# Convolution by taps: the fourth tap of 5 of 14 tiles a chunk goes from VectorE to ScalarE and GpSimd

## What is computed

```python
def _short_conv(x, w):                       # 4 taps, causal, per channel
    xp = jnp.pad(x, ((0, 0), (cs - 1, 0), (0, 0)))
    y = sum((xp[:, i:i + t, :] * w[:, i] for i in range(cs)))
    return jax.nn.silu(y)

q = _short_conv(x @ Wq, conv_q)              # 8 heads of 128 channels
k = _short_conv(x @ Wk, conv_k)              # 3 x 8 heads
v = _short_conv(x @ Wv, conv_v)              # 3 x 8 heads
# per token, 3 Householder steps of the state S (128 x 128 a head), then o = q S
S = S * jnp.exp(gt)[..., None, None]
for i in range(nh):
    kS = jnp.einsum('bhd,bhde->bhe', ki, S)
    S = S + bi[..., None, None] * (ki[..., None] * (vi - kS)[:, :, None, :])
```

## Time and profile before

| | |
|---|---|
| three runs | 8217.16, 8217.32, 8226.03 us (median 8217.32) |
| profiled execution | 8217.97 us, its span 8215.9 us |
| busy, share of the span | TensorE 90%, VectorE 79%, ScalarE 67%, GpSimd 50% |
| mean granted TensorE clock | 0.944 of full |
| stretches | 0 to about 150 us preparation; then the attention to about 6900 us; then the experts |
| one iteration of the loop (8 chunks) | 218.42 us |

### The profile page before, as it was taken

How to read it: one execution, slowest core, us unless ns; L and a number is a source line. 1 busy time by engine, 2 the same in 40 slices (tenths; PEclk the granted TensorE clock), 3 DMA queues, 4 the chain that set the end, 5 groups by cost and what they waited for, 6 DMA issues and landing times. The chain is left out here.

```text
span 8215.9 us, 426591 instructions
## 1 busy us (share of the span) xinstructions
PE 7423.3 (90%) x155940; PEld 6296.7 (77%) x155940; DVE 6459.2 (79%) x22300; ACT 5469.5 (67%) x20343; POOL 4117.8 (50%) x6333
## 2 busy tenths in 40 slices
PE   5889999999999999999999899999989999889999
PEld 3777777777787777777777777777777777757777
DVE  4888888888888888888888888888888888623333
ACT  3777777777777777777777777777777777533333
POOL 0555555555555555555555555555555555511111
PEclk6899999999999999999999999999999999889999
DMA  2000000000000000000000000000000000010000
GB/s 90 8 10 9 10 9 10 9 10 9 10 10 9 10 10 10 9 10 9 10 9 10 9 10 9 10 9 10 10 9 10 9 10 10 7 32 8 10 8 8
DMA packets 283626, 97.69 MB, mean 12 GB/s; under 512 B 226097, under 2 KB 276545, under 8 KB 281153
## 3 DMA queue, kind: packets, MB, share of 16 engines
q1 hardware_dynamic: 281408, 68.93, 3.8%
HBM read 52.08 MB, written 16.78 MB: 8 GB/s over the span
## 5 line engine op out<-in xcount | busy, mean ns | idle before, releaser
L819 DVE SCALAR_TENSOR_TENSOR CY<-PP,CWV,CY 128x128 f32<-128x128 f32 x4608 | 1585.5, 344 | 148.6 <-ACT CY L736 68.7
L819 DVE SCALAR_TENSOR_TENSOR CY<-PP,CWK,CY 128x128 f32<-128x128 f32 x4608 | 1581.4, 343 | 98.0 <-ACT CY L736 24.3
L1031 POOL TENSOR_TENSOR UM<-U,C 32x256 f32<-32x256 f32 x1536 | 1104.8, 719 | 120.2 <-POOL UM L1031 19.6
L1024 POOL TENSOR_TENSOR Y<-U,C 32x256 f32<-32x256 f32 x768 | 554.0, 721 | 1075.6 <-DVE UQ L912 1035.4
L550 PE MATMUL PI<-T,WB 32*32 32x32 f32 x49152 | 749.6, 196 | 303.2 <-DVE T L828 301.1
L550 PEld LDWEIGHTS PI<-T,WB 32*32 32x32 f32 x49152 | 639.0, 111 | 466.3 <-issue 403.2
L530 PE MATMUL PP<-XT,WV 128*128 128x131 f32 x3072 | 750.8, 328 | 188.5 <-issue 124.7
L530 PE MATMUL PP<-XT,WK 128*128 128x131 f32 x3072 | 783.6, 340 | 81.3 <-DVE CY L819 81.2
L736 ACT ACTIVATE CY<-PP,CWK 128x128 f32<-128x128 f32 x1536 | 564.4, 367 | 398.5 <-PE PP L530 387.4
L1004 POOL TENSOR_TENSOR S<-R,BETA 96x4 f32<-96x4 f32 x512 | 101.3, 198 | 1392.4 <-DVE R L872 1392.2
L736 ACT ACTIVATE CY<-PP,CWV 128x128 f32<-128x128 f32 x1536 | 567.2, 369 | 339.3 <-PE PP L530 328.0
(11 more groups left out here) (228 smaller groups left out, 18910.8 us busy)
## 6 DMA issues: line engine op xcount, KB each, us to landing
EX<-exd SPq DMA_DIRECT2D x768, 32.0 KB
exd<-EXS SPq DMA_DIRECT2D x16, 512.0 KB, 2.6
XR<-in_L_attn_x SPq DMA_DIRECT2D x65, 64.0 KB, 3.1
XL<-in_L_attn_x SPq DMA_DIRECT2D x16, 256.0 KB, 2.8
XRES<-in_L_attn_x SPq DMA_DIRECT2D x64, 64.0 KB, 2.7
x<-X SPq DMA_DIRECT2D x64, 64.0 KB, 3.1
XI<-x SPq DMA_DIRECT2D x16, 256.0 KB, 2.9
out<-OUT SPq DMA_DIRECT2D x16, 256.0 KB, 2.3
```

Source lines behind the costliest of these rows:

```text
L819: dve.scalar_tensor_tensor(CY[:, m % RING], ptile(m)[:, s:s + P], taps_of(m)[:, s:s + 1], CY[:, m % RING], ALU.mult, ALU.add).then_inc(tap ...
L1024: pool.tensor_tensor(Y1[r, :, :], U[r, par, :, r], over(first[r, :], [BK, NHEAD, BK], 1), ALU.mult).then_inc(seed_sb, 1)
L1031: pool.tensor_tensor(UM[r, lv], U[r, par, :, r], over(merge[lv][r, :], [BK, NHEAD, BK], 1), ALU.mult).then_inc(made, 1)
```

## The change

Of the 14 tiles of a chunk, those of slots 0, 1, 5, 6 and 7 (`OFF`) lose VectorE's third step. ScalarE makes tap 3 times its weight out of PSUM into a new ring buffer `CZ` of four tiles, just ahead of the instruction that makes `CY`. VectorE's tap 2 then counts for two on `taps_sb`. GpSimd adds `CZ` to `CY` (`last_tap`), and ScalarE's silu of these tiles waits for that (`tap3_sb`). GpSimd's additions stand at three places of its chunk: tile 0 after `YF` and `RS`; tile 1 after `FB`; tiles 5, 6 and 7 after `RT` and ahead of the wait for `UQ`.

```diff
+OFF = (0, 1, 5, 6, 7)
+NOFF = len(OFF) * CPS
...
+        ZRING = 4
+        assert NOFF % ZRING == 0
+        CZ = sb("CZ", [P, ZRING, P])
...
+        tap3_sb = sem("tap3_sb")
...
+        def off_rank(m):
+
+            return len(OFF) * (m // SLOTS) + OFF.index(m % SLOTS)
...
                             need(act, kqv_sb, T - RING + 1)
+                            if k in OFF:
+                                act.activation(CZ[:, off_rank(m) % ZRING], ptile(m)[:, 3:3 + P], ACT.Copy, scale=taps_of(m)[:, 3:4])
                             act.activation(CY[:, m % RING], ptile(m)[:, 0:P], ACT.Copy, scale=taps_of(m)[:, 0:1]).then_inc(tap0_sb, 1)
...
-                            act.wait_ge(taps_sb, 3 * (T + 1))
+                            if m % SLOTS in OFF:
+                                act.wait_ge(tap3_sb, NOFF * j + off_rank(m) + 1)
+                            else:
+                                act.wait_ge(taps_sb, 3 * (T + 1))
...
-                                             ALU.mult, ALU.add).then_inc(taps_sb, 1)
+                                             ALU.mult, ALU.add).then_inc(taps_sb, 2 if s == 2 and m % SLOTS in OFF else 1)
...
-                        if taps:
+                        if taps and m % SLOTS not in OFF:
                             tap(j, m, 3)
...
+                def last_tap(i, m):
+                    pool.wait_ge(taps_sb, 3 * (TILES * i + m + 1))
+                    pool.tensor_tensor(CY[:, m % RING], CY[:, m % RING], CZ[:, off_rank(m) % ZRING], ALU.add).then_inc(tap3_sb, 1)
...
+                    if known(i, 0, NSC):
+                        for k in OFF:
+                            if k in (0,):
+                                last_tap(i, SLOTS * c + k)
                     if c == 2 and known(i - 2, 0, NSC):
...
+                            if k in (1, 2):
+                                last_tap(i, SLOTS * c + k)
                     if do_prep:
...
                         pool.tensor_tensor(RT[:, :], SSE[:, :], half4[:, :], ALU.pow).then_inc(rt_sb, 1)
+                    if known(i, 0, NSC):
+                        for k in OFF:
+                            if k in (5, 6, 7):
+                                last_tap(i, SLOTS * c + k)
+                    if do_prep:
                         pool.wait_ge(u_sb, 2 * prep + 2)
```

## The result

| | before | with the change |
|---|---|---|
| median | 8215.61 us (20 runs) | 8237.47 us (20 runs) |
| profiled execution | 8217.97 us | 8232.63 us |
| ratio, same chip | | 1.0026, 95% interval 1.0015 to 1.0038 |
| on a second chip | 8239.56 us (23 runs) | 8243.41 us (12 runs): 1.0004, 0.9993 to 1.0015 |

The change costs 22 us on one chip, which can be told there, and 4 us, nothing that can be told, on the other. The forecast was 8229 us, +0.14%.

A forecast was written before the change was run, and what follows sets the result against it. VectorE was taken to pace TensorE until slot 3, ScalarE from slot 4 to 7. Terms by kind of chunk, -28.8 + 16.2 + 23.3, summed to +10.7 us, hence 8229 us; the 8-in-10 range was 8110 to 8305.

The forecast's parts named there:

- Two clocks, VectorE to slot 3 and ScalarE from slot 4 to 7: TensorE follows VectorE until slot 3, ScalarE's unbroken row in slots 4 to 7, and itself sets the time after.
- The tap, 0.39 us in the stream: Each VectorE tap removed ahead of T saves 0.39 us; tiles 0 and 1 together give 0.78 us where VectorE is late.
- CZ, 0.25 us: Each added ScalarE multiplication costs 0.25 us in its unbroken row, priced from similar 128-column PSUM reads.
- Rival B: In ScalarE's row CZ costs 0.39 us, lengthening it by 1.17 us a chunk: 8309 us; chance 0.18.
- The sum by kind: Gains and costs added by kind of chunk, c = 0 to 3 and after the back edge: +10.7 us in all.
- The first KD of c = 3, costed at one CZ: In c = 3 only the first KD binds TensorE, adding 0.25 us against a 0.78 us gain: -0.53 us.
- The other signs: Next-profile signs: T's wait falls to a third in c = 1 and 3; KD waits of 0.3 to 0.7 us appear.
- The taps of tiles 5 to 7, costed at nothing: Taps removed in slots 6 to 8 gain nothing, since TensorE follows ScalarE there; otherwise up to 1.17 us a chunk.
- rival C: Shared access: each of five GpSimd additions holds VectorE 0.21 us, giving 8296 us; chance 0.06.
- D: Rival: GpSimd's sum comes late for tile 5's silu, by 0.3 us in each chunk: 8295 us; chance 0.05.
- Rival A: ScalarE's row has slack, CZ is absorbed in slots 5 to 7, front gains stay: 8117 us; chance 0.33.
- I am wrong altogether if the gap in c = 2 shrinks so far that the clock holds: If TensorE's 2.28 us gap in c = 2 shrank enough, the slow stretch would end and time fall below 8117 us.

The follow-up runs named there:

- experiment 1: The change for tiles 0 and 1 only, against the kernel before: 8107.54 us, 0.9836.
- experiment 2: The change for tiles 5, 6 and 7 only, against the kernel before: 8334.94 us, 1.0108.
- experiment 4: The kernel before with the fourth tap of the five tiles left out of the computation, nothing put on ScalarE or GpSimd: 8061.37 us, 0.9787.
- experiment 9: The kernel before with FA behind T in c = 2 and ScalarE's output squares moved to slot 11 of each chunk: 8021.18 us, 0.9756.
- experiment 10: The kernel of experiment 9 plus the change for tiles 0 and 1 only: 7850.46 us, 0.9546 of the kernel before.
- Experiment 3: The kernel before plus ScalarE's five CZ multiplications, never read; VectorE makes all taps, GpSimd adds nothing: 8413.08 us, 1.0207.
- experiment 5: The unaltered change measured again on the second chip, against the kernel before: 8243.41 us, 1.0004.
- experiment 12: The kernel of experiment 9 plus the change for all five tiles: 7903.78 us, 0.9595 of the kernel before.
- experiment 6: The change with each GpSimd addition made twice, once into an unread buffer: 8243.5 us, 1.0009 of the kernel before.
- experiment 7: The kernel before with FA of chunks c = 2 moved behind the inversion step T: 8079.98 us, 0.9818.
- 8: 7, tiles 0, 1: The kernel of experiment 7 plus the change for tiles 0 and 1 only: 8046.05 us, 0.9775 of the kernel before.

## Why the prediction was right, point by point

- **Two clocks, VectorE to slot 3 and ScalarE from slot 4 to 7.** Shown by experiments 1 and 2, where each half moves one wait and leaves the other.
- **The tap, 0.39 us in the stream.** c 0 to 1 holds two taps of the chunk c = 1; it fell by 0.85 us in experiment 1, 0.87 in 4 and 0.87 between 9 and 10, so 0.43 a tap, a tenth over the term.
- **CZ, 0.25 us.** 0.25 in the mean over all of them; three lengthen ScalarE's row by 0.77. Rival B (0.39) falls. At TensorE three CZ cost 0.85 us in c 0 to 1 of experiment 2, 0.28 each, again a tenth over the term. With 0.28 and 0.43 in place of 0.25 and 0.39 the sum would be about +15 us (an estimate): the two errors nearly cancel, which is luck, since with CZ alone at 0.28 the recorded formula gives +28. Experiment 3 cost 172 us instead of 144, so all of CZ together is a fifth dearer than my terms; the time at 1.2 GHz grew there from 21.6 to 28.6 us an iteration, which they don't have.
- **The sum by kind.** Put on the table's intervals (the back of a chunk and the front of the next), the terms are:

| interval | forecast | measured | again, experiment 5 |
|---|---|---|---|
| 0 to 1 | +0.75 - 0.78 = -0.03 | +0.04 | +0.01 |
| 1 to 2 | +0.75 + 0.11 = +0.86 | +1.08 | +1.08 |
| 2 to 3 | 0 - 0.78 = -0.78 | -0.58 | -0.35 |
| 3 to 0 | +0.25 - 0.26 = -0.01 | -0.19 | -0.20 |
| 3 to 0, over the edge | +0.25 | -0.09 | +0.17 |

  The first says most: in an interval that shows no change at all, two effects of 0.8 us cancel. The others are off by 0.1 to 0.4 us with both signs. Over an iteration they make +0.8 us, and +1.4 in the repeat, where the terms make +0.3. That the total came so near is in part luck, these misses cancelling: 0.1 us a chunk is 26 us.
- **The first KD of c = 3, costed at one CZ.** Too high. TensorE's products do not wait for KD in 3 to 0 after the change, and experiment 2, where only this term acts, has +0.12 us there instead of +0.25.
- **c = 2.** FA's wait grew by 0.44 us (0.50 forecast), the gap by 0.20 (0.11 forecast). The clock drop stayed, but not "as it is": the time at 1.2 GHz in c = 2 is 15.4 us an iteration before, 16.5 after and 17.7 in the repeat. The forecast had no term for that.
- **The other signs.** In the mean of the table's iterations T's wait fell from 1.1 us to 0.25 in c = 1, and from 1.23 to 0.45 in c = 3, and is 2.49 instead of 2.28 in c = 2: as forecast. The weight loads of each Gram product wait 0.5 us for KD in c = 0 and 1 (0.3 to 0.7 forecast). ScalarE's busy time grew by 280 us, 8.8 an iteration (10 forecast). GpSimd's wait for UQ fell by 1.8 us a chunk (1.35 forecast).
- **The taps of tiles 5 to 7, costed at nothing.** In the change this held: in c 2 to 3 TensorE waits 0.63 us for taps before and after, and 0.64 in experiment 4, which has these taps left out and no CZ. It does not hold in every kernel. Where the clock holds in c = 2 and T comes early there, TensorE waits 1.31 us for them with tiles 0 and 1 moved (experiment 10) and 0.77 with all five (experiment 12). Which of the two conditions opens that wait no run separates; with a full clock alone (experiment 9) it is 0.64.
- **GpSimd costs nothing.** Shown by experiment 6, with twice the additions. Rivals C and D had 11% together. The taps of v took 346 ns after and 344 before, with GpSimd 57% busy instead of 50%. The Trainium skill, SBUF — State Buffer, "Who interferes with whom", says that a VectorE instruction with at most one SBUF input, outside the 2-port modes, does not contend with GpSimd. The trace agrees for the taps. The warning of the Trainium skill in Perfetto Trace Analysis, "Optimizing Scalar/DVE Operations", that moving work between the two might not help, was not borne out in the time by these additions; one instruction of VectorE did feel them, as told below.
- **Rival A (ScalarE's row not the bound)** had 33% and falls: the KD wait is there. It was overweighted: the 0.07 us between KD and the Gram product was no coincidence.
- **"I am wrong altogether if the gap in c = 2 shrinks so far that the clock holds".** It did not with this change, but experiments 7 and 9 show that this was the larger lever. The shorter gap and the held clock together gave 2.4%, and it made the relief of tiles 0 and 1 worth 2.1% instead of 1.6%.

## What to carry to other kernels

Before an instruction is moved to an engine with a lower busy share, look for the stretch in which that engine sets the next start. Here ScalarE, 67% busy before the change, bounds four slots of 14 in two kinds of chunk, and the same edit gains 134 us in two tiles and costs 89 us in three others. Split such a change by place and keep the half that pays. And where a gap is followed by a stretch at a lower clock, take the instruction that waits for another engine out of the row ahead of the gap before anything is offloaded.

## What the hardware showed that I had not expected

**The clock after a short gap.** The table counts, over the same 28 iterations, the chunks c = 2 in which the granted clock fell to 0.50 of full around the gap ahead of T.

| kernel | TensorE's gap, us | chunks with a fall, of 56 |
|---|---|---|
| 3: CZ unused | 2.78 to 2.81 | 52 |
| the change | 2.48 to 2.50 | 47 |
| 1: tiles 0, 1 | 2.32 to 2.49 | 35 |
| before | 2.28 to 2.30 | 52 |
| 2: tiles 5 to 7 | 2.28 to 2.29 | 45 |
| 4: tap left out | 1.97 to 2.00 | 43 |
| 8: 7, tiles 0, 1 | 1.71 to 1.89 | 37 |
| 7: FA late | 1.35 to 1.37 | 15 |
| 9: squares late too | 1.02 to 1.12 | 0 |

The falls get rarer with a shorter gap, but the gap alone does not decide: within one kernel chunks with and without a fall have the same gap, experiment 1 has fewer than experiment 4, and in c = 3, where the gap is 1.22 to 1.26 us, experiment 2 has 8 falls and experiment 9 none. What decides is open. The scatter of the runs goes with it. On one chip nine runs of the kernel before lie within 37 us, five of experiment 9 within 8 and five of experiment 10 within 6. The five of experiment 7, with falls in some iterations, lie within 57.

**Who is held by whom.** OG reads two SBUF buffers. Experiment 10, VectorE and then GpSimd, c = 2:

```profile
2935.55 0.60 DVE L918 SCALAR_TENSOR_TENSOR OG<-OSB,FB,GSIL 128x128 f32<-128x128 f32 x2
...
2936.70 1.29 DVE L918 SCALAR_TENSOR_TENSOR OG<-OSB,FB,GSIL 128x128 f32<-128x128 f32 x2
...
2933.39 0.20 POOL L1034 TENSOR_TENSOR KDS<-R,TAIL 96x4 f32<-96x4 f32 x1
...
2935.60 0.36 POOL L1034 TENSOR_TENSOR KDS<-R,TAIL 96x4 f32<-96x4 f32 x1
...
2936.49 0.89 POOL L1040 TENSOR_TENSOR EM<-E,C 96x384 f32<-96x384 f32 x1
```

A pair of OG takes 0.60 us, but 1.29 beside GpSimd's mask of 384 columns; and GpSimd's small KDS takes 0.36 us beside OG where it takes 0.20 beside a BZ. The taps, which read PSUM and one SBUF buffer, never show this: in no kernel of the study is one longer than 0.354 us, while OG reaches 0.66 in the kernel before and 0.83 in experiment 10. So the contention of rival C exists on this chip, in an instruction that the change doesn't edit but does reach: OG's mean is 358 ns before, 392 after and 445 with doubled additions. It cost nothing that can be told there. In experiment 10 it lies in slots 6 to 8 of c = 2, where TensorE waits for VectorE's taps; how much of that wait is OG's stretching no run separates.
